# Attention behind a long convolution: scales of q, k and v from a bound, four conv groups a tile, the second product in halves, and the last weight sums on VectorE

## The reference, cut to what matters

```python
# x: (4, 256, 32, 32); b = 4 batches, 256 channels, t = 1024 positions, 4 heads of 64
xf  = layer_norm_over_channels(x).reshape(4, 256, 1024)
qkv = conv1d(group_norm(xf, gamma, beta), qkv_w, 16 taps) + qkv_b     # 768 channels out
q, k, v = split(qkv.reshape(16, 192, 1024))                           # 16 = batch x head
w   = softmax((q * 64**-0.25)^T (k * 64**-0.25))                      # 1024 x 1024 per head
h   = w v
h   = conv1d(h, proj_w, 5 taps) + proj_b
x   = x + xf + h
t   = tokens(x)
x   = t + table_step(layer_norm(t))    # one-hot digits found, shifted and added as +2.0 marks
```

## Time and profile before

| | |
|---|---|
| median of 3 runs | 1208.02 us (1207.48, 1208.02; a third lies far off at 1765.97) |
| the profiled execution | 1204.91 us, of which 1202.8 us are the span from the first instruction to the last |
| mean granted TensorE clock | 0.944 of full speed |
| PE | 1027.8 us busy (85%), 6760 matmuls |
| DVE / ACT / POOL | 763.5 (63%) / 653.9 (54%) / 222.6 us (19%) |
| chain that ended last | PE 44%, DVE 25%, ACT 11%, issue 11%, DMA 6% |

### The profile page before, as it was taken

The page is one execution under the profiler, slowest core; times in us unless marked ns, Lnnn a source line. Parts: engine busy times, 40 slices in busy tenths (PEclk is TensorE's granted clock), DMA queues, the critical chain, the costliest instruction groups (busy, mean ns, idle before and its releaser), DMA issues.

```text
span 1202.8 us, 17282 instructions
## 1 busy us (share of the span) xinstructions
PE 1027.8 (85%) x6760; PEld 670.4 (56%) x6760; DVE 763.5 (63%) x1359; ACT 653.9 (54%) x1073; POOL 222.6 (19%) x164
## 2 busy tenths in 40 slices
PE   2877589989998986977988899899989997888865
PEld 1655455655566554545545466656566565666644
DVE  5998658545854565566556465456447564687857
ACT  5574456545653655646656455455436464656612
POOL 2644203100310130040040010000000003043211
PEclk9998889999999997988998999999999999898978
DMA  6220144753476344626733366436444663344522
GB/s 249 65 113 1 54 110 85 177 97 63 87 163 144 71 97 111 135 45 144 164 71 59 70 130 130 80 53 150 88 79 93 175 148 72 89 82 94 108 59 71
DMA packets 284512, 122.53 MB, mean 102 GB/s; under 512 B 268304, under 2 KB 270736, under 8 KB 283536
## 3 DMA queue, kind: packets, MB, share of 16 engines
q1 hardware_dynamic: 284432, 121.44, 45.2%
HBM read 34.24 MB, written 15.87 MB: 42 GB/s over the span
## 4 chain that ended last, share of the span: by engine, by line
PE 44%; DVE 25%; ACT 11%; issue 11%; DMA 6%; POOL 2%; SPq 1%; POOLq 0%; DVEq 0%; ACTq 0%
PE cP L1023 10%; PE psV L1103 9%; PE cM L1023 9%; PE cQ L1023 8%; DMA arena<-arena 5%; DVE smx L1447 4%; PE psS L1067 4%; PE psT L1067 3%; ACT arena L885 3%; DVE arena L1428 2%; ACT arena L897 2%; DVE W L1212 2%; DVE W L1219 2%; POOL wsum L525 1%; DVE arena L1303 1%
## 5 line engine op out<-in xcount | busy, mean ns | idle before, releaser
L1023 PE MATMUL cQ<-U,W 128*128 128x256 f16 (+1 forms) x1536 | 224.6, 304 | 20.7 <-issue 11.1
L1023 PE MATMUL cP<-U,W 128*128 128x256 f16 (+1 forms) x1536 | 223.7, 302 | 14.3 <-issue 11.8
L1023 PE MATMUL cM<-U,W 128*128 128x256 f16 (+1 forms) x1536 | 222.6, 301 | 12.4 <-DVE U L1248 7.4
L1023 PEld LDWEIGHTS cQ<-U,W 128*128 128x128 f16 x1536 | 151.1, 99 | 91.2 <-issue 16.9
L1447 DVE TENSOR_REDUCE smx<-psS 128x1 f32<-128x1024 f32 x64 | 77.9, 1218 | 188.2 <-PE psS L1067 188.2
L1023 PEld LDWEIGHTS cP<-U,W 128*128 128x128 f16 x1536 | 149.7, 98 | 83.4 <-issue 20.6
L1023 PEld LDWEIGHTS cM<-U,W 128*128 128x128 f16 x1536 | 149.5, 97 | 82.0 <-issue 10.0
L1103 PE MATMUL psV<-arena 128*128 128x512 f16 x512 | 138.4, 432 | 56.6 <-DMA arena<-arena 56.5
L1428 DVE SCALAR_TENSOR_TENSOR arena<-arena,smx 128x1024 f16<-128x1024 f32 x128 | 173.4, 1355 | 6.4 <-ACT arena L897 5.9
L878 ACT ACTIVATE smx<-smx,esc 128x1 f32<-128x1 f32 x128 | 37.3, 291 | 248.2 <-DVE smx L1447 248.2
L897 ACT ACTIVATE arena<-arena,smx 128x1024 f16<-128x1024 f32 x128 | 147.0, 1148 | 4.3 <-DMA arena<-arena 0.2
(11 more groups left out here) (207 smaller groups left out, 1186.4 us busy)
## 6 DMA issues: line engine op xcount, KB each, us to landing
staging<-w_qkv SPq DMA_DIRECT2D x20, 512.0 KB, 5.2
kept_u<-U SPq DMA_DIRECT2D x4, 2077.0 KB, 10.6
U<-kept_u SPq DMA_DIRECT2D x16, 519.2 KB, 4.5
arena<-x_tok SPq DMA_DIRECT2D x8, 512.0 KB, 6.7
arena<-arena SPq DMA_DIRECT2D x16, 256.0 KB, 3.6
W<-x_tok SPq DMA_DIRECT2D x4, 1024.0 KB, 6.1
out_tok<-W SPq DMA_DIRECT2D x3, 1024.0 KB, 4.6
kept_h<-arena SPq DMA_DIRECT2D x4, 514.0 KB, 5.4
```

The source lines that it names most:

```text
L1023: last = mm(out, W[:, j, wl, c, wat + tap, :], U[:, slot, ul, c, at:at + width], start=(c == 0 and tap == 0 and wl + ul == 0), stop=(c == ...
```

## The change

Scales of q, k and v: VectorE takes once the largest of |gamma|, |beta| and |bias| and forms a bound; each of the six weight tiles gets one scale from the sum of squares of its weights and that bound (`y_scale`), for all four batches. `finish_y`, `scale_y` and `y_top` go. Groups: the two common parts share one bank (g = 1), so a tile has four groups and one `common_copy` of 512 columns. Second product: eight halves of 16 matmuls of 256 columns, at slots 4, 6, ... 16, the last behind the transposes of v at the step's end. `heads` becomes two pieces in neighbouring slots. Weights: the tables name, for each engine, its own slot for each piece (squares, sum, rounding, remainder), in tiles 3 to 5 one slot apart and in an order of parts of each tile's own, and there the sums are made by VectorE. Some transfers take other places in the queue. In the last conv step the residual is prepared one slot later and GpSimd's part is named on its own.

```diff
-GROUPS = 5
+GROUPS = 4
@@ tables: one slot per engine and piece
-            3: table(tile_weights(3, 0, 1, 2, 2, 3, 4, 5, 5, 6, 6, 7, 8),
-                     tile_weights(4, 13, 14, 15, 15, 15, 16, 16, 17, 17)),
-            4: table(tile_weights(4, no, no, no, no, no, no, no, no, no, 0, 1, 1),
-                     tile_weights(5, 6, 7, 8, 8, 9, 10, 11, 12, 12, 13, 14, 14), [(16, ("pads", 0))]),
+        ACT_BEFORE = {
...
+            3: {3: [("hi", 3, 0, 1)], 5: [("hi", 3, 2, 3)], 6: [("hi", 3, 8)], 7: [("hi", 3, 4, 5)], 8: [("hi", 3, 9)],
+                9: [("hi", 3, 6, 7)], 10: [("hi", 3, 10)], 11: [("hi", 3, 11)], 14: [("squares", 4, 0)],
+                15: [("squares", 4, 1)], 17: [("hi", 4, 0, 1, 8)]},
+            4: {0: [("hi", 4, 10)], 1: [("hi", 4, 4, 6)], 2: [("hi", 4, 9)], 3: [("hi", 4, 2, 3)], 5: [("hi", 4, 5, 7, 11)],
+                4: [("squares", 5, 0)], 7: [("squares", 5, 1)], 9: [("hi", 5, 0, 1)], 10: [("hi", 5, 2, 3)],
...
+        DVE_AT = {
...
+            3: {2: [("sums", 3, 0)], 3: [("lo", 3, 0, 1)], 4: [("sums", 3, 1)], 5: [("lo", 3, 2, 3)],
+                6: [("lo", 3, 8), ("sums", 3, 2)], 7: [("lo", 3, 4, 5)], 8: [("lo", 3, 9), ("sums", 3, 3)],
+                9: [("lo", 3, 6, 7)], 10: [("lo", 3, 10)], 11: [("lo", 3, 11)], 15: [("wadd", 4)],
+                16: [("wscale", 4), ("sums", 4, 0)], 17: [("lo", 4, 0, 1, 8), ("sums", 4, 1)]},
+            4: {0: [("lo", 4, 10)], 1: [("lo", 4, 4, 6)], 2: [("lo", 4, 9), ("sums", 4, 2)], 3: [("lo", 4, 2, 3)],
+                4: [("sums", 4, 3)], 5: [("lo", 4, 5, 7, 11)], 6: [("yscale", 4)], 7: [("wadd", 5)],
+                8: [("wscale", 5), ("sums", 5, 0)], 9: [("lo", 5, 0, 1), ("sums", 5, 1)],
...
@@ SyncE's queue
-                wait(sp, "pv_done", 4 * k + u // 4)
+                wait(sp, "pv_done", 8 * k + u // 2 - 1)
-                    if u == 1 and 1 <= k <= NB:
+                    if u == 2 and 1 <= k <= NB:
                         keep_h(k - 1)
-                    if k == 1 and 11 <= u < 15:
+                    if k == 1 and 9 <= u < 13:
-                        load_w(3, [u - 11])
+                        load_w(3, [u - 9])
-                    if k == 2 and 8 <= u < 12:
-                        load_w(4, [u - 8])
-                    if k == 3 and u in (1, 2):
-                        load_w(5, [2 * u - 2, 2 * u - 1])
+                    if k == 2 and u in (11, 12):
+                        load_w(4, [2 * u - 22, 2 * u - 21])
+                    if k == 3 and u in (1, 5):
+                        load_w(5, [0, 1] if u == 1 else [2, 3])
@@ GpSimd
-                    if i in (3, 9, 16):
+                    if i in (3, 9, 15):
                         add_common(n, i // 6, 0)
-                    if i in (5, 11, 17):
+                    if i in (4, 10, 16):
                         add_common(n, i // 6, 1)
@@ ScalarE
-            def common_copy(n, p, j, q):
-                act.wait_ge(S["conv_done"], GROUPS * (3 * n + j) + 2 * q + 2)
-                a(ap[:, q, :], bank_of(j, 2 * q + 1)[:, 0:QUART], ACT.Copy,
+            def common_copy(n, p, j):
+                act.wait_ge(S["conv_done"], GROUPS * (3 * n + j) + 2)
+                a(ap[:, :, :].rearrange("p q i -> p (q i)"), bank_of(j, 1)[:, :], ACT.Copy,
                   scale=isc[:, 3 * p + j:3 * p + j + 1]).then_inc(S["a_done"], 1)
-                    if conv and i in (14, 15):
-                        qk_hi(3 * n + 1, 0, i - 14)
+                    if conv and i in (12, 13):
+                        qk_hi(3 * n + 1, 0, i - 12)
@@ TensorE
+            def tops(n, i):
+
+                if (n, i) == (2, 17):
+                    pe.wait_ge(S["e_done"], 16 * 2)
+                    weight_top(3, psS)
+                if (n, i) == (3, 16):
+                    pe.wait_ge(S["e_done"], 16 * 3 - 1)
+                    weight_top(4, psS)
+                if (n, i) == (4, 8):
+                    pe.wait_ge(S["y1_done"], 3 * 4 + 1)
+                    weight_top(5, bank_of(0, 3))
...
+            def second_product(k, h):
+
+                gi, at = h // 2, h % 2 * QUART
+                for u in (2 * h, 2 * h + 1):
+                    pe.wait_ge(S[f"turned{u % 4}"], 16 * (4 * k + gi + 1))
+                if h == 0:
+                    pe.wait_ge(S["vl_done"], 2 * k + 2)
+                if h % 2 == 0:
+                    wait(pe, "hs_done", 4 * k + gi)
+                for s in range(8):
+                    for l in range(2):
+                        last = mm(psV[:, at:at + QUART], vT[:, s, gi // 2, :], probT[:, 8 * l + s, at:at + QUART],
+                                  start=(s + l == 0), stop=(s + l == 8))
+                last.then_inc(S["pv_done"], 1)
...
-                    if attn and i in PV_SLOTS:
...
+                    if attn and 4 <= i <= 16 and i % 2 == 0:
+                        second_product(k, i // 2 - 2)
+                    if attn and not conv and i == 17:
+                        second_product(k, 7)
...
                     for s in range(8):
                         last = tr(psT[:, s * P:(s + 1) * P], yv[:, s * P:(s + 1) * P], ident[:, :])
                     last.then_inc(S["vt_done"], 1)
+                    if attn:
+                        second_product(k, 7)
@@ VectorE
+            def bounds():
+
+                ch = Chain(dve, "c_u", 0, 2)
+                ch.step(v.reduce_max(amr[:, 4:6], bank[1][:, P:3 * P].rearrange("p (k o) -> p k o", o=P), X))
+                ch.done(v.scalar_tensor_tensor(ybound[:, 0:1], amr[:, 4:5], 2.0 * P * T * NB, amr[:, 4:5], ALU.mult, ALU.mult))
+                v.scalar_tensor_tensor(ybound[:, 1:2], amr[:, 5:6], 2.0, amr[:, 5:6], ALU.mult, ALU.mult) \
+                    .then_inc(S["yb_done"], 1)
+                ch.end()
+
+            def y_scale(m):
+
+                ch = Chain(dve, "c_y", m, 5)
+                dve.wait_ge(S["yb_done"], 1)
+                dve.wait_ge(S["wsc_done"], m + 1)
+                ch.step(v.tensor_scalar(ysq[:, 0:1], top[:, m:m + 1], ybound[:, 0:1], ybound[:, 1:2], ALU.mult, ALU.add))
+                pow2(ch, ysq[:, 0:1], QK, ysc[:, m, 0:1], ysc[:, m, 1:2], squared=True)
...
+            def w_sums(m, i):
...
+                    v.tensor_tensor(wsum[:, at % 2], pair[0], pair[1], ALU.add).then_inc(S["wsum_done"], 1)
-                v.tensor_reduce(am[:, 2:3], y[:, :], X, ALU.max, apply_absolute_value=True).then_inc(S["yam_done"], 1)
-                    if conv and i in (15, 16):
-                        qk_lo(i - 15, 0, 2 * n)
+                    if conv and i in (13, 14):
+                        qk_lo(3 * n + 1, 0, i - 13)
```

More of the change, by code:

```diff
@@ L238, in rstd @@
             ch.step(v.tensor_tensor(out, q, s, ALU.mult))
-        WSTAGES = ("wmax", "wadd", "wtop", "wscale", "wsum0", "wsum1", "wsum2", "w00", "w01", "wsum3", "w10", "w11")
-        def tile_weights(m, *slots):
-            return [(slot, (kind, m)) for slot, kind in zip(slots, WSTAGES) if slot is not None]
-        def table(*lists):
-            t = {}
-            for slot, entry in sorted(sum(lists, []), key=lambda e: e[0]):
-                t.setdefault(slot, []).append(entry)
-            return t
@@ new lines, in build, with sums_of @@
+        ORDER = ((0, 1, 2, 3, 4, 5, 8, 6, 7, 9, 10, 11), SUM_FIRST, SUM_FIRST, (0, 1, 2, 3, 8, 4, 5, 9, 6, 7, 10, 11),
+                 (0, 1, 8, 10, 4, 6, 9, 2, 3, 5, 7, 11), (0, 1, 2, 3, 4, 5, 8, 6, 7, 9, 10, 11))
+        def sums_of(m):
+            return [part for part in ORDER[m] if part < SUMS]
+        POOL_AT = {
+            1: {0: [("ring", 0)], 1: [("first", 2)], 3: [("fine", 2, 0)], 4: [("fine", 2, 1)], 6: [("fine", 2, 2)],
+                7: [("fine", 2, 3)]},
+            2: {1: [("first", 3)], 3: [("fine", 3, 0)], 4: [("fine", 3, 1)], 6: [("fine", 3, 2)], 7: [("fine", 3, 3)]},
+            4: {17: [("pads", 0)]},
+        }
@@ L300, in build, with place @@
         LAST = max(LATE) + 1
-        def sum_part(h):
-            return h if h < 6 else h + 2
+        def place(m, part):
+            return PARTS * m + ORDER[m].index(part) + 1
         def sum_taps(h):
@@ L533, in extra @@
+            def extra(kind, k, tile=None):
+                if kind == "sums":
+                    sums(k, tile)
+                if kind == "first":
+                    first_low(k)
+                if kind == "fine":
+                    fine_low(k, tile)
                 if kind == "ring":
@@ L735, in qk_hi @@
+                    last_stage(kind, k, *which)
+                if kind == "first":
+                    first_high(k)
+                if kind == "fine":
+                    fine_high(k, *which)
+                if kind == "squares":
+                    squares(k, *which)
+                if kind == "hi":
+                    w_hi(k, *which)
             def qk_hi(run, hd, part):
-                act.wait_ge(S["ysc_done"], run + 1)
+                m = run % TILES + TILES * (run // (NB * TILES))
@@ L738, in qk_hi @@
```

(24 more changed lines are left out.)

650 lines of the change are left out of this document (309 added, 341 removed), and 2 rows, old and new, of the table ACT_BEFORE.

## The result

The changed kernel takes 1124.36 us (median of 4, 1124.24 to 1124.58); its ratio to the kernel before is 0.931, 95% interval 0.9287 to 0.9332. Two of the four times of the kernel before (1765.97 and 2647.45 us) lie far off and are left out of that ratio. Forecast were 1111 us and a range of 1088 to 1145.

A forecast was written before the change was run, and what follows sets the result against it. TensorE was taken to bound steps 1 to 7 wherever not kept waiting; 89 us gained there plus 12 at the end make 101, giving 1107 us by median, plus 4 for dense slots: 1111, range 1088 to 1145.

The forecast's parts named there:

- the limit: Steps 1 to 7: TensorE sets the pace, its own work being 107.1 us a step at full clock.
- the 1.5 us left for a late eighth half: End of each conv step: allowance for a late VectorE uncovering some of the 2 to 3 us cover, 1.5 us a step.
- Halves at the conv rate: Second product: 1024 matmuls of 256 columns at 3.51 against 3.45 us, costing 2 us in all.
- I leave 4 us there with its restart: Step 4, slot 8: TensorE stands for tile 5's late second load half and its sum of squares; 4 us.
- the rival (a): Steps 3 and 4: VectorE takes GpSimd's place, about half of 50 us stays, 1136 us; chance 0.15.
- step 0 is a long VectorE chain which changes its order and hardly its length: 0: Step 0: no change in length expected, within 4 us either way.
- That makes 12: Last step: 12 us gained, from scale wait 8, half of the last product 3, VectorE's short waits 1.
- VectorE's short waits between the two halves of a head's output go, 1: Last step: VectorE's waits between the output halves of a head disappear, gaining 1 us.
- I am wrong if: Refuting signs: halves over 120 ns each, additions averaging over 1 us, or the eighth half still waiting over 3 us.
- the three sources: TensorE's losses: last second product awaiting transposes, third group awaiting `ysc_done`, weight conversion passed between engines in steps 3 and 4.
- the second one: Third group of a tile waits for `ysc_done`; in step 3 TensorE idles 6.12 us; the bound removes this wait.
- the 4 added for dense slots: Whole kernel: 4 us added because slacks were read from slots never this dense, taking 1107 to 1111 us.

The follow-up runs named there:

- A: Changed kernel with the second half of weight tile 5's load issued behind turn 4 of step 4 instead of turn 5: 1117.9 us, ratio 0.926.
- J: Changed kernel, tile 4's last three parts converted earlier, tile 5's second load half behind turn 3, sum of squares ahead of head's sum: 1115.3 us.
- C: Changed kernel with the 24 additions of weight tiles 3 to 5 back on GpSimd, in the same slots: 1119.6 us, ratio 0.927.
- I: Changed kernel with batch 3's norm chain and scaling earlier in step 0, and the copy of k ahead of the kept U: 1117.2 us, ratio 0.925.
- L: Changed kernel with I, J, most of C, last-step projection pairs earlier, tile 5's parts 9 to 11 earlier, last-step head's copy and sum first: 1098.0 us.
- F: Kernel before, from the second step on without TensorE's transposes spreading maxima of y or its waits for scales: 1199.2 us, ratio 0.994.
- D: Changed kernel with the second product whole again, 16 matmuls of 512 columns at slots 5, 9, 13 and 17: 1156.1 us, ratio 0.958.
- E: As C, with addition, rounding and remainder of a part in one slot, each at its end: 1146.7 us, ratio 0.950.
- B: As A, with tile 4's last three buffer-sharing parts rounded and subtracted in slot 4, their additions in slot 3: 1121.9 us, ratio 0.929.

## Why the prediction was right or wrong

The measured time lies inside the range; of the 97 us forecast between the medians, 84 came. The steps say where they are missing.

**Right: the limit, and steps 1, 2, 3 and 5 to 7.** A step's work of 107.1 us is the floor. Step 1 was put at 114.4 and took 113.3, step 3 at 111.4 and took 112.5. Steps 2, 5, 6 and 7, put at 108.9 each, took 107.2 to 107.3: the 1.5 us left for a late eighth half was not needed, as no half of steps 1 to 7 waited. Halves at the conv rate held: 1.75 us for 16, so 109 ns a matmul. The Trainium skill's "TensorE: Matmul & The Clock Gate", section "Back-to-back issue gap", has about 131 ns at 512 columns, where the trace shows 216, and between its two figures the prediction estimated 98 at 256; the trace goes by the columns.

**Wrong: the load of tile 5, priced at 4 us in "I leave 4 us there with its restart".** The place was named as it came, TensorE idle at slot 8 of step 4. Its size was not: step 4 took 130.2 us, and the terms gave 115.4. The place measured 14.7 us: 12.0 of wait, and 1.3 and 1.4 more than usual for the two groups of matmuls behind it. The step that failed is the chain behind the landing. Its 6.7 us from the start of the squares to TensorE (squares, exponentials, reciprocal, the head's sum, the addition) were listed in part and not added up: 541.5 + 5.2 + 6.7 would have been 553, which is 10 us of wait by itself. The load, priced by the page's median from issue to landing, 5.2 us, adds the other 2: the squares start 7.2 us after its first issue. A and J show the place to be the cause, J with 7.9 us net off step 4. The rest of its excess, unit 4's wait, tile 5's last remainders and the lower clock behind some of them, falls under the rival (a) in kind, that step 4's slots are too full. C shows, though, that taking the additions off VectorE does not shorten the step; what would stays open.

**Wrong by 6.4 us: "step 0 is a long VectorE chain which changes its order and hardly its length: 0".** That is outside its own "within 4 either way". The order was the point. The norm chain of batch 3 stands at the end of that list, behind a scale chain; with it moved ahead, and ScalarE's scaling of that batch (I), step 0 is 151.6.

**Wrong by 5 us: "That makes 12" for the last step**, which gave 7.0. The scale wait went, as forecast. But "VectorE's short waits between the two halves of a head's output go, 1" has the sign wrong: TensorE now needs psV three times before VectorE has read the last head's output from it (7.7 us in all), and L, which puts that reading first in its slots, takes these waits away. The last half still waited 5.7 us and ran at the lower clock. This is the one item of the list "I am wrong if" that came true, the eighth half waiting over 3 us, once of eight; all second products wait 13.4 us where under 12 was named.

**Right in the sum, not one by one: the three sources.** They were priced each by its own idle time. F shows that TensorE's waits of the second one, 23.9 us, are worth 7 when they alone go; D that the halves are worth 32, mostly not in the quiet steps from which their price was read; and E that the places of additions and roundings are worth 27. As all were removed together, the sum came near; a sum for one of them would not have. The relief of VectorE by the bound and the four groups were run in no experiment by themselves. The move of the additions was costed rightly in itself (0.69 forecast, 0.72 measured) and was a loss of 4.8 us as a choice (C).

By profiled times the forecast was 97 us of gain, with the 4 added for dense slots, and 80.5 came. Missing are 14.8 in step 4, 6.4 in step 0 and 5.0 in the last; against them stand 6.5 gained in the quiet steps and the 4, and under 1 us of small ones. That the total is nearer than its parts is luck: errors of both signs met in it.

## What to carry to other kernels

When an engine waits on a transfer, add up the whole chain behind its landing on every engine, in queue order, up to the engine that stands: here the chain was 6.7 us and the surcharge of the transfer over its median 2. When engines wait for each other by slots, idle times named in the profile are no separate savings: removing one alone pays only where nothing else is late at the same place, so look for what else meets there. And a piece that passes from engine to engine wants its stages apart in the lists (here the addition a slot ahead, the rounding at its slot's start, the remainder at its end) before it wants a faster engine: 27 us came from the places here, and the faster addition cost 4.8.

Two rows of a view can mislead: a row that merges several instructions (B) hides the wait between them, and a wait put down to one engine (L) can be that engine's own wait for another.

## What the runs showed of the hardware that was not expected

- The two transfers of the second half of tile 5's load landed 5.8 and 6.7 us after their issue in the changed kernel, 6.3 and 7.0 in A, but 4.0 and 4.9 in J, against a median of 5.2 to 5.4 over the twenty of each run. What makes the difference was not tested.
- With the additions on GpSimd, VectorE's low part of a probability tile (128x1024) takes 1415 ns in the mean of steps 3 and 4, with them on VectorE 1274; over 32 of them that is 4.5 us, less than the 16.4 that the additions had taken.
- After 12.0 us without work TensorE ran 12 matmuls of 256 columns in 2.77 us in place of 1.48, and the next 16 in 3.33 in place of 1.91; from 555.4 to 561.3 the granted clock is 0.52. After waits of 1.0 us (D) a product of 16 took its usual 3.61.
